# Dealt mixture of experts: row loads seven tiles ahead, a reordered queue in the second shared block, and routed rows scaled by ScalarE and added by GpSimd

## The reference

```python
x = L0_attn_x                                                # (2, 1024, 256) float32
x = _layernorm(x + _L0_attn_ref(x, ...))                     # causal attention, 16 heads of 128
x = _layernorm(x + _L0_ffn_ref(x, ...))                      # 8 experts, top 2, and a shared expert
x = _layernorm(x + _L1_attn_ref(x, ...))                     # grouped attention, 16 heads of 16, 4 key groups
x = _layernorm(x + _L1_ffn_ref(x, ...))                      # 16 experts, top 6, and a shared expert
```

```python
def _L0_ffn_ref(x, gate_w, w_gate, w_up, w_down, sw_gate, sw_up, sw_down, shared_gate_w):
    top_w, top_i = jax.lax.top_k(softmax(x @ gate_w.T), 2);  top_w = top_w / top_w.sum(-1)
    expert_out = (silu(x @ w_gate[e]) * (x @ w_up[e])) @ w_down[e]      # 176 wide, for each e
    moe_out = sum of the two chosen expert_out, weighted by top_w
    shared_out = (silu(x @ sw_gate) * (x @ sw_up)) @ sw_down            # 704 wide
    return moe_out + shared_out * sigmoid(x @ shared_gate_w)
```

## Time and profile before

| | |
|---|---|
| median of 3 runs | 2228.19 us (2222.27 to 2229.81) |
| the profiled execution | 2240.19 us, its span 2238.5 us |
| mean granted TensorE clock over the span | 0.958 |
| busy share of the span | PE 92%, DVE 64%, ACT 54%, POOL 28% |
| routed tiles "e0" | 1025.4 to 1264.1 us of the span |
| shared block of half 1, "f2" | 1264.1 to 1366.0 us |

### The profile page before, as it was taken

The page is one execution under the profiler, slowest core; times in us unless marked ns, Lnnn a source line. Parts: engine busy times, 40 slices in busy tenths (PEclk is TensorE's granted clock), DMA queues, the critical chain, the costliest instruction groups (busy, mean ns, idle before and its releaser), DMA issues. The chain is left out here.

```text
span 2238.5 us, 34436 instructions
## 1 busy us (share of the span) xinstructions
PE 2064.7 (92%) x12163; PEld 1583.0 (71%) x12163; DVE 1433.0 (64%) x2885; ACT 1199.7 (54%) x2456; POOL 616.5 (28%) x731
## 2 busy tenths in 40 slices
PE   8999999999999999986665778999999999999998
PEld 6888888887887888775555655333334578778886
DVE  5776666667667666654323456799997456655555
ACT  5666666666555666553212233588888634434333
POOL 3444444443334455542201040000000012222221
PEclk9999999999999999997778887699999999999999
DMA  2300000000000000041222130110000111111111
GB/s 72 128 20 20 20 20 20 20 20 13 20 20 19 25 29 19 27 104 55 88 62 76 46 80 22 27 23 20 19 23 2 33 30 45 48 43 43 50 46 59
DMA packets 74222, 86.91 MB, mean 39 GB/s; under 512 B 12443, under 2 KB 54086, under 8 KB 74054
## 3 DMA queue, kind: packets, MB, share of 16 engines
q1 hardware_dynamic: 70982, 76.32, 12.2%
q0 software_dynamic: 3072, 8.39, 1.2%
HBM read 58.32 MB, written 18.35 MB: 34 GB/s over the span
## 5 line engine op out<-in xcount | busy, mean ns | idle before, releaser
L1133 POOL TENSOR_TENSOR a_pr<-a_pr,a_rinv 128x512 f32<-128x512 f32 (+3 forms) x384 | 312.5, 828 | 463.7 <-DVE a_rinv L1390 463.6
L91 PE MATMUL psum<-xh,g_hi_gu 128*128 128x512 f32 x744 | 308.0, 414 | 13.1 <-PEq L59 5.3
L2817 ACT ACTIVATE a_pt<-psum 128x512 f32<-128x512 f32 x512 | 276.2, 597 | 71.8 <-PE psum L2717 52.1
L2836 DVE TENSOR_REDUCE x_m_negm<-psum 128x1 f32<-128x1024 f32 x240 | 290.8, 1224 | 27.4 <-PE psum L2702 25.3
L93 PE MATMUL psum<-xh,g_lo_gu 128*128 128x512 f32 x744 | 294.4, 396 | 0.0
L92 PE MATMUL psum<-xl,g_hi_gu 128*128 128x512 f32 x744 | 293.7, 395 | 0.0
L1481 POOL TENSOR_TENSOR g_lo_gu<-g_raw_gu,g_hi_gu 128x512 fp32r<-128x512 f32 x62 | 80.0, 1291 | 667.4 <-ACT g_hi_gu L1477 667.4
L1295 ACT ACTIVATE a_pr<-psum,a_negm 128x128 f32<-128x128 f32 (+7 forms) x256 | 190.0, 742 | 116.3 <-DVE a_negm L1380 112.7
L1302 ACT ACTIVATE a_pth<-psum 128x512 fp32r<-128x512 f32 (+3 forms) x384 | 174.7, 489 | 112.0 <-PE psum L1199 108.4
L1397 DVE TENSOR_TENSOR a_ptl<-psum,a_pth 128x512 fp32r<-128x512 f32 (+3 forms) x384 | 201.3, 552 | 2.1 <-ACT a_pth L1302 1.7
L2717 PE MATMUL psum<-x_queries_qq,x_ks 49*128 49x512 f32 x512 | 193.8, 459 | 1.6 <-ACT a_pt L2817 0.5
(11 more groups left out here) (401 smaller groups left out, 4744.7 us busy)
## 6 DMA issues: line engine op xcount, KB each, us to landing
g_raw_gu<-in_gu SPq DMA_DIRECT2D x60, 256.0 KB, 2.8
g_raw_gu<-in_qkv SPq DMA_DIRECT2D x32, 256.0 KB, 2.9
f_raw_dn<-in_down SPq DMA_DIRECT2D x60, 128.0 KB, 2.0
xs<-a_mask SPq DMA_DIRECT2D x2, 2944.0 KB, 10.8
e_xt<-xs SPq DMA_DIRECT2D x46, 128.0 KB, 2.2
ys<-e_yb SPq DMA_DIRECT2D x46, 128.0 KB, 1.7
a_wvr<-in_qkv SPq DMA_DIRECT2D x32, 128.0 KB, 2.3
a_wor<-in_o SPq DMA_DIRECT2D x32, 128.0 KB, 2.1
```

Source lines behind the costliest of these rows:

```text
L91: pe.matmul(out, a_hi, b_hi, start=first, stop=False)
L1133: pool.tensor_tensor(x, x, rinv[:, j:j + 1].to_broadcast([P, count * P]), ALU.mult).then_inc(p_done, 1)
L2817: act.activation(pt[:, s % SLOTS, g, :], st_ps[:, n % 3, :], ACT.Exp, scale=1.0 / HD1).then_inc(exp_done, 1)
L2836: dve.tensor_reduce(negm[:, u % 2, g * NQ + q:g * NQ + q + 1], mx_ps[:, bank, :, :], AX.XY, ALU.max, negate=True).then_inc(mx_taken, 1)
```

## The change

There are four edits, which touch the stages f0, e0 and f2.

1. **Row loads.** `AHEAD` goes from 4 to 7. Four of the eight row slots move from `routed` to `Experts` (`xa`), and SP loads the first four tiles of half 0 at the end of f0's list (`first_rows`).
2. **Scaling and adding.** The DVE's `gs` is gone. ACT scales the four pieces of a group by their shares (four activations), and POOL adds the copies in one instruction of 512 columns (`add`). `nf` is split: `nf` writes the sum, and a new task `ns`, one step later, takes the statistics.
3. **Plan of e0.** The gathers come earlier (`GATHER`), `gs` every three steps from 29, `nf` from 31, `ns` from 32, `std` and the first `xn` at 42, the second at 43, and half 0's `BACK` at 43 to 46.
4. **f2.** SP loads weight tiles 2 and 3 ahead of the queries. The projections move to K = 0 and 1, `FirstMaxima` to K = 2 to 5 (they had 3 to 6).

```diff
 class GatheredNorm(NormHalf):
-        self.before = b * self.TILES
+        self.before = b * self.GROUPS
+    def add(self, pool, s):
+        g = self.slots[s]
+        pool.wait_ge(self.scaled, 4 * (self.before + s + 1))
+        pool.tensor_tensor(g[:, 0:2, :], g[:, 0:2, :], g[:, 2:4, :], ALU.add).then_inc(self.added, 1)
+
     def scalar(self, act, t, ring):
-        if t[0] not in ("nf", "gs"):
+        if t[0] == "gs":
+            s = t[1]
+            g, w = self.slots[s], self.deal.share
...
+            act.wait_ge(self.got[s], 16 * 2 * TOP0 * (self.b + 1))
+            for k in range(TOP0):
+                for q in range(2):
+                    act.activation(g[:, 2 * k + q, :], g[:, 2 * k + q, :], ACT.Copy,
+                                   scale=w[:, k, 2 * s + q:2 * s + q + 1]).then_inc(self.scaled, 1)
...
     def vector(self, dve, t, ring):
         if kind == "gs":
-            for q in range(2):
-                dve.tensor_scalar(g[:, q, :], g[:, q, :], w[:, 0, 2 * s + q:2 * s + q + 1], None, ALU.mult).then_inc(self.scaled, 1)
-            for q in range(2):
-                dve.wait_ge(self.scaled, self.before + 2 * s + q + 1)
-                dve.scalar_tensor_tensor(out=g[:, q, :], in0=g[:, 2 + q, :], scalar=w[:, 1, 2 * s + q:2 * s + q + 1], in1=g[:, q, :],
-                                         op0=ALU.mult, op1=ALU.add).then_inc(self.added, 1)
+            return
...
 class Experts:
+    def first_rows(self, sp, deal, xs):
+        sp.wait_ge(deal.scattered, deal.all_scattered())
+        for i in range(self.EARLY):
+            sp.dma_start(self.xa[:, i, :], xs[i * P:(i + 1) * P, :]).then_inc(self.x_in[i], 16)
...
 def shared_half(...):
+            if not experts:
+                load(2)
+                load(3)
             for o in begins:
                 if isinstance(o, FirstMaxima):
                     o.queries.first(sp, o.side, ring)
             for K in range(2, NT):
-                load(K)
+                if K >= 4 or experts:
+                    load(K)
...
             if experts:
                 experts.load(sp, 2 * NT - 2)
+                experts.first_rows(sp, router, xs)
...
+            if gathered is not None:
+                for s in range(NormHalf.GROUPS):
+                    gathered[0].add(pool, s)
 def routed(...):
-        GATHER = [NT + 4 + 2 * n for n in range(NormHalf.TILES)]
+        GATHER = [NT + 3 + 3 * n // 2 for n in range(NormHalf.TILES)]
-            AHEAD = 4
-            for i in range(AHEAD):
+            AHEAD = XSLOT - 1
+            for i in range(EARLY, AHEAD):
                 load(i)
...
                 gathered.gather(pool, ys[0], n)
+                if n >= 3 and n % 2:
+                    gathered.add(pool, n // 2 - 1)
+            gathered.add(pool, NormHalf.GROUPS - 1)
 # the plans
-                        plan[M0 + 9 + 4 * s] = tasks(n1a, [("gs", s), ("nf", s)])
-                    plan[2 * M0] = tasks(n1a, [("std",), ("xn", 0)])
-                    plan[2 * M0 + 1] = tasks(n1a, [("xn", 1)])
+                        plan[M0 + 6 + 3 * s] = tasks(n1a, [("gs", s)])
+                        plan[M0 + 8 + 3 * s] = tasks(n1a, [("nf", s)])
+                    for s in range(NormHalf.GROUPS):
+                        plan[M0 + 9 + 3 * s] = plan.get(M0 + 9 + 3 * s, []) + tasks(n1a, [("ns", s)])
+                    plan[M0 + 19] = tasks(n1a, [("std",), ("xn", 0)])
+                    plan[M0 + 20] = tasks(n1a, BACK[:1] + [("xn", 1)])
+                    for s in range(1, NormHalf.GROUPS):
+                        plan[M0 + 20 + s] = tasks(n1a, BACK[s:s + 1])
...
                     for n in range(m0.COUNT):
-                        plan[3 + n // 4, n // 2 % 2, n % 2] = [(m0, (0, n)), (m0, (1, n))]
+                        plan[2 + n // 4, n // 2 % 2, n % 2] = [(m0, (0, n)), (m0, (1, n))]
```

More of the change, by code:

```diff
@@ L664, in vector @@
         if kind == "gs":
[L665 to L669, removed]
-            for q in range(2):
-                dve.tensor_scalar(g[:, q, :], g[:, q, :], w[:, 0, 2 * s + q:2 * s + q + 1], None, ALU.mult).then_inc(self.scaled, 1)
-            for q in range(2):
-                dve.wait_ge(self.scaled, self.before + 2 * s + q + 1)
-                dve.scalar_tensor_tensor(out=g[:, q, :], in0=g[:, 2 + q, :], scalar=w[:, 1, 2 * s + q:2 * s + q + 1], in1=g[:, q, :],
-                                         op0=ALU.mult, op1=ALU.add).then_inc(self.added, 1)
[L676 to L686, removed]
+            return
+        if kind == "ns":
+            n = 2 * t[1]
+            y = self.yT[:, :, self.tokens(t[1])]
+            dve.wait_ge(ring.emptied, ring.count((self.name, ("nf", t[1]))))
             for q in range(2):
@@ L692, in vector @@
                 dve.bn_aggr(self.mv[:, n + q, :], self.stats[:, n + q, :]).then_inc(self.mv_done, 1)
+        elif kind == "nf":
+            s = t[1]
+            n = 2 * s
+            y, o = self.yT[:, :, self.tokens(s)], ring.bank(key)
+            dve.wait_ge(self.added, self.before + s + 1)
+            dve.wait_ge(ring.filled, ring.count(key))
+            for q in range(2):
+                i = dve.scalar_tensor_tensor(out=y[:, q, :], in0=o[:, q * D:(q + 1) * D], scalar=self.deal.sg[:, n + q:n + q + 1],
+                                             in1=self.slots[s][:, q, :], op0=ALU.mult, op1=ALU.add)
+            i.then_inc(ring.emptied, 1)
         else:
@@ L1939 @@
     PIECES = 4
+    XSLOT, EARLY = 8, 4
     def __init__(self, ph, name, w, raw):
@@ L1946, in __init__ @@
         self.dl = ph.sb(f"{name}_dl", [P, 2, NE, D], F32R)
+        self.xa = ph.sb(f"{name}_xa", [P, self.EARLY, D])
+        self.x_in = [ph.sem(f"{name}_x_in{s}") for s in range(self.XSLOT)]
         self.raw_in = [ph.sem(f"{name}_raw_in{s}") for s in range(2)]
@@ L2319, in routed @@
     N = B * NT
-    XSLOT, YSLOT = 8, 3
+    XSLOT, EARLY, YSLOT = Experts.XSLOT, Experts.EARLY, 3
     GATE = INTER
     with Phase(nc, tag, psum) as ph:
-        xt = ph.sb("xt", [P, XSLOT, D])
+        late = ph.sb("xt", [P, XSLOT - EARLY, D])
+        xt = [experts.xa[:, s, :] for s in range(EARLY)] + [late[:, s, :] for s in range(XSLOT - EARLY)]
         sxh = ph.sb("sxh", [P, 2, DT, P], F32R)
@@ L2336, in routed @@
         side_ps = ph.ps([P, 2, CH])
-        x_in = [ph.sem(f"x_in{s}") for s in range(XSLOT)]
+        x_in = experts.x_in
         x_turned = ph.sem("x_turned")
@@ L2369, in load @@
                     sp.wait_ge(y_kept, i - XSLOT + 1)
-                sp.dma_start(xt[:, i % XSLOT, :], xs[half][r * P:(r + 1) * P, :]).then_inc(x_in[i % XSLOT], 16)
+                sp.dma_start(xt[i % XSLOT], xs[half][r * P:(r + 1) * P, :]).then_inc(x_in[i % XSLOT], 16)
             def store(i):
@@ L2532, in keep_y @@
                     dve.wait_ge(y_out[i % YSLOT], 16 * (i // YSLOT))
-                dve.tensor_tensor(yb[:, i % YSLOT, :], y_ps[:, i % 2, 0:D], xt[:, i % XSLOT, :], ALU.add).then_inc(y_kept, 1)
+                dve.tensor_tensor(yb[:, i % YSLOT, :], y_ps[:, i % 2, 0:D], xt[i % XSLOT], ALU.add).then_inc(y_kept, 1)
             keep_x(0)
@@ L3061, in program @@
                     x1 = QKVHalf(s, "x1", 1, wqkv, kv, khi, klo, xh, xl, ident, "n1b").into(qhi[1], qlo[1], ks[1], vs[1])
[L3062 removed]
+                    in_turn(nc, "p1", counters, psum, tasks(n1b, [("nf", 0), ("ns", 0), ("nf", 1), ("ns", 1)]) + tasks(x0, [("pj", 1, 0)]) +
+                            tasks(n1b, [("nf", 2), ("ns", 2), ("nf", 3), ("ns", 3)]) + tasks(x0, [("pj", 1, 1)]) +
                             tasks(n1b, [("root",)] + BACK) + tasks(x1, PROJECT), (x1, wo, rw1, queries),
```

27 lines of the change are left out of this document (14 added, 13 removed).

## The result

The changed kernel takes 2109.93 us (median of four runs, 2106.45 to 2114.72) against 2226.01 us (four runs, 2222.27 to 2229.81): a ratio of 0.948, 95% interval 0.9453 to 0.9507. The gain is 116 us, where 116 was forecast, and the time is 2 us from the forecast of 2112.

What follows compares the result with a forecast made beforehand. The prediction took PE's 89.3 us of waits for row loads to bound the routed tiles. Gains of 110 us there (238.7 to 129) and 6 us in f2 make 116 us off 2228.2: 2112 us, range 2096 to 2154.

Steps and rivals of the forecast that it cites:

- The stall of the row loads: Routed tiles: PE's 89.3 us of waits for row loads fall to under 5 us with loads seven tiles ahead.
- The step: Routed tiles: one tile step without waits lasts 2.32 us at the high clock; 46 steps make 107 us.
- The rest of the stage: Routed tiles: start, dealing, scaling and adds, end and drain add 4.5 + 5 + 3 + 4 + 7 us to the steps.
- The seven dealing steps: Routed tiles: half 1's seven dealing tasks on DVE lengthen their steps by 5 us, bounds 0 to 8.
- The last sixteen steps with gathers and scalings: Routed tiles: ACT's scaling and POOL's adds, with the transposes of `nf`, cost 3 us, bounds 0 to 6.
- forecast 4 + 7: End of the routed tiles: 4 us for the norm's root, table loads and scalings, 7 us for the drain.
- The start: Opening of the routed tiles: first gate and up 2.5 us in, two low-clock steps +2 us, together 4.5 us.
- f2: Shared block of half 1: 96 us against 101.9, 6 us gained, between a loss of 6 and a gain of 18.
- The new wait: f2 at K = 2: PE stands 14 us because the small query and key loads queue behind tile 3's down weights.
- the case of 2154 us: Rival, routed tiles: low clock for half of the steps, 42 us come back, 2154 us; chance 0.17.
- Late gathers and results: Rival, routed tiles: ACT's scaling waits for gathers and delays work behind it, 25 us come back, 2137 us; chance 0.15.
- Row loads limited by rate: Rival, routed tiles: queue rate limits the loads, so going seven ahead brings nothing; 2237 us, chance 0.02.

Runs made afterwards that it cites:

- b5: Kernel before the change with only the row loads altered, five tiles ahead instead of four; 2137.68 us, ratio 0.9602.
- aq: Changed kernel with another order of SP's list in f2, the small query and key loads ahead of tile 3's down weights; 2093.47 us, ratio 0.944.
- b7: Kernel before the change with only the row loads altered, seven tiles ahead instead of four; 2118.62 us, ratio 0.9534.
- a4: Changed kernel with the row loads back at four tiles ahead, all its other edits kept; 2217.88 us, ratio 0.9971.
- adve: Changed kernel with scaling and adding of the routed rows back on DVE, no add on POOL; 2112.01 us, ratio 0.949.
- abest2: As abest, and with the first four row loads issued at the start of the routed stage; 2089.82 us, ratio 0.94.
- anorm: Changed kernel with the end of half 0's norm in the two drain steps instead of the last full-tile steps; 2113.83 us, ratio 0.9502.
- after2: The changed kernel, unaltered, timed again in the third set; 2115.64 us, ratio 0.9521 to the kernel before.
- alate2: The same kernel as alate, run again in the third set beside the unaltered changed kernel; 2115.24 us, ratio 0.9513.
- abest: Changed kernel with aq's order of SP's list in f2 and the four scalings one or two places earlier on ACT; 2090.38 us, ratio 0.9406.
- alate: Changed kernel with the first four row loads back at the start of the routed stage; 2100.65 us, ratio 0.9446.
- aspread: Changed kernel with the next block's weight loads and their roundings twelve steps later in the routed tiles; 2108.22 us, ratio 0.9488.

## Why the prediction was right

- *The stall of the row loads.* The wait was to go as long as a load lands within 6.95 us, and it went. With the measured step of 2.13 us the limit was 2.2 + 3 x 2.13 - 2.25 = 6.3 us, and b5 shows landings of up to 3.7 us where I reckoned with 2.2. So some 2.6 us of the margin were left.
- *The step.* 2.32 us was too much; measured are 2.10 to 2.19 us, most of them 2.13. The row of before counts from the first matmul to the end of the last, which is 0.32 us, and 0.16 of that overlap the next matmul as soon as one follows. Over 46 steps that is (2.32 - 2.13) x 46 = 9 us, where I took off 1.5.
- *The rest of the stage.* 129 us predicted, 124.0 measured, which is 98 for 46 steps of 2.13 and 26 for everything else, where 23.5 were forecast. The seven dealing steps took 18.6 us instead of 7 x 2.13 = 14.9, so 3.7 (forecast 5). The last sixteen steps with gathers and scalings took 39.4 us instead of 34.1, so 5.3 (forecast 3). From the last transposes at 1134.28 to f2 at 1147.57 passed 13.3 us, of which some 2.1 are a step's own, so 11.2 (forecast 4 + 7). A step of 5.89 us near 1050, 3.8 above a plain one, was not foreseen at all, and seventeen steps behind it were 2.4 us longer than plain ones together. The start, forecast at 4.5, cost nothing: four steps on from the first transposes PE is 8.2 us into the stage, and four plain steps are 8.5. The stage came out 1 us under the 125 to 135 us that were to show the forecast right.
- *f2.* 96 us predicted, 98.1 measured. The new wait was forecast at 14 us and came at 13.72; the reason was the right one too, since aq takes it away by the order of the queue alone. Tile by tile K = 0 to 6 lasted 12.2, 11.0, 29.5, 12.0, 12.0, 11.9 and 9.6 us, where 14.3, 10.2, 29, 12.2, 12.2, 10.5 and 7.5 were forecast. K = 0 was 2.1 us too much and K = 6 2.1 us too little, and they cancel. K = 6 is 1245.69 - 1236.07 = 9.6 us: I had ACT's four scalings and POOL's add in the sum, but not that they stand behind 2.1 us of copies. (It is counted, as the 15.7 us of before were, from the last pair of maxima of K = 5; the row at 1350.35 is that pair, not the first of four of K = 6.)
- *The rivals.* The clock was 0.96 in the routed tiles, so the case of 2154 us did not come. The Trainium skill, "TensorE: Matmul & The Clock Gate", section "Part 1: The HAM clock gate", says that the clock follows how busy the array has been of late. This trace agrees in the routed tiles (busy 90%, clock 0.96), and the stretch of 0.50 with PE busy throughout, above, does not fit it. Late gathers and results cost 5.3 us at the most, not 25. Row loads limited by rate: b7 rules that out.
- *The sum.* 129 - 124 = 5 us too little gained in one stage, 2 us too much in the other. The agreement within 2 us is partly luck: the two errors and 2 us of difference between the medians of before all but cancel, and the kernel after itself took 2109.93 us in one set and 2115.64 us in another.

## What to carry to other kernels

Price a prefetch by the landing time in the loop that it is to make, not in the one that it cures, and leave room above it. 2.2 us became 2.2 to 3.7, and five tiles ahead, with a lead of some 2.1 us, left a fifth of the gain. In an in-order DMA list look at each wait for what stands behind it: moving 24 small loads ahead of one wait was worth 16.9 us of f2, when all of the change but the lead brought 4 us (a4). And before a difference of two spans is explained, compare a part of the program that the change leaves alone.

## What the runs showed of the hardware

- *A low clock with PE busy.* In the traces of before, b5, adve and abest2 the granted clock fell to 0.50 some 13 to 14 us into the grouped attention and stayed there for 27 to 34 us, PE being busy all the time. In a4 and anorm it fell there too, but had risen again within ten us, and in the other eight traces the same instructions kept it. In all six it fell right behind one or two waits of PE of 0.35 to 0.40 us for a maximum on DVE, and the kernel after has two such waits at the same place and kept its clock. So what decides it isn't shown. It costs 13.4 us by the two spans above. In abest2 the profiled run with it took 2106.48 us, one more 2106.98, and the four others 2087.14 to 2090.50 us.
- *A stall of three engines at once.* Ahead of the transposes of tile 12 PE, DVE and ACT all stood for 1 to 2.6 us with no semaphore behind it that the profile shows, and the step took 4.9 to 6.1 us, in after, b7, aq, after2, alate2, abest and abest2. POOL went on (in after, scatters at 1050.18, 1051.44 and 1053.88). In the four kernels of the second set it was missing, though among them is alate, which is alate2. A second one came near tile 31 in after2 and alate2 (4.48 and 4.10 us). From the first load to f2, or from 1.06 us ahead of the first transposes where the loads left earlier, the routed stage is 124 to 128 us in the traces with it and 116 to 120 in those without. The one step is under half of that difference. Nor does the stall explain the 9 us of alate, since adve, anorm and aspread have none either and stand 8 to 13 us above alate. Its cause stays open: the second set also ran on another chip, and the arrival of instructions was not looked at.
